# A routed FFN's tail: where three pairs of query tiles are normalised and their squared norms taken

## The reference

```python
q = (hidden_states @ Wq + bq).reshape(B, S, H, QD)      # 8 heads of 64
q = (q - mean) / jnp.sqrt(var + EPS_BN) * bn_gamma + bn_beta   # over all tokens and heads
q0 = _l2norm(q[..., :HALF]); q1 = _l2norm(q[..., HALF:])
s0 = jnp.einsum('bshq,kq->bshk', q0, k0); s1 = ...      # 32 keys each
ts0, ti0 = jax.lax.top_k(s0, 4); ts1, ti1 = jax.lax.top_k(s1, 4)
# 16 sums of a first and a second score, softmax over them: weights of 16 of 256 experts
eh = gelu(down[idx] . hidden_states)
out = sum over the chosen experts of up[idx] * eh * w
```

## Time and profile before

| what | value |
|---|---|
| time, median of 3 runs | 415.46 us (415.35 to 417.52) |
| the profiled execution | 416.85 us, its span 415.1 us |
| busy share: PE, DVE, ACT, POOL | 96%, 72%, 59%, 52% |
| the FFN's tail over the 16 tiles | about 331 to 413 us of the span |

### The profile page before, as it was taken

One profiled execution on the slowest core, in us unless ns is written; L12 is line 12 of the kernel. 1 busy time (PEld: TensorE's weight loads), 2 busy tenths in 40 slices (PEclk: granted clock), 3 DMA queues, 4 the chain that ended last, 5 costly groups with the idle time before them and its releaser, 6 DMA issues. The chain is left out here.

```text
span 415.1 us, 7901 instructions
## 1 busy us (share of the span) xinstructions
PE 397.8 (96%) x2582; PEld 367.0 (88%) x2582; DVE 297.7 (72%) x1104; ACT 245.7 (59%) x539; POOL 215.9 (52%) x208
## 2 busy tenths in 40 slices
PE   2999999999999999999999999999999999999877
PEld 1788888899899999999999999999778998999766
DVE  4889777786366676457565555565695999799996
ACT  3687759354465655456573534443566887779462
POOL 2588999764263224334333212000147767989994
PEclk9999999999999999999999999999999998999999
DMA  7800223003422222231232100000100000000101
GB/s 223 299 0 3 76 56 101 8 7 127 109 64 64 55 81 77 59 80 52 58 98 59 54 2 2 0 2 0 28 1 2 0 3 1 27 28 26 41 25 65
DMA packets 19993, 21.38 MB, mean 52 GB/s; under 512 B 3181, under 2 KB 16625, under 8 KB 19953
## 3 DMA queue, kind: packets, MB, share of 16 engines
q1 hardware_dynamic: 18832, 19.96, 16.4%
q10 hardware_dynamic: 1120, 0.92, 0.8%
HBM read 18.78 MB, written 2.10 MB: 50 GB/s over the span
## 5 line engine op out<-in xcount | busy, mean ns | idle before, releaser
L847 DVE TENSOR_TENSOR att_pTl<-context_pR,att_pTh 128x512 fp32r<-128x512 f32 x64 | 37.4, 586 | 26.4 <-ACT att_pTh L759 26.1
L1191 POOL TENSOR_TENSOR ffn_prod<-ffn_first,ffn_near 128x1024 f32<-128x1024 f32 (+1 forms) x29 | 54.1, 1882 | 2.1 <-DVE ffn_first L1608 2.1
L866 DVE TENSOR_REDUCE att_mx<-keep_pQ 128x1 f32<-128x402 f32 x64 | 35.3, 567 | 24.2 <-PE keep_pQ L77 24.2
L759 ACT ACTIVATE att_pTh<-context_pR 128x512 fp32r<-128x512 f32 x64 | 32.4, 516 | 9.8 <-PE context_pR L1018 9.0
L1762 PE MATMUL ffn_pT<-keep_ident,ffn_prod 128*128 128x128 f32 x240 | 29.5, 277 | 4.3 <-POOL ffn_prod L1191 4.3
L1762 PEld LDWEIGHTS ffn_pT<-keep_ident,ffn_prod 128*128 128x128 f32 x240 | 27.3, 143 | 6.5 <-DVE ffn_hT L1641 4.8
L223 POOL TENSOR_TENSOR gru_z<-gru_z,gru_g 128x512 f32<-128x512 f32 x16 | 28.8, 1801 | 8.0 <-DVE gru_g L428 8.0
L1018 PE MATMUL context_pR<-keep_ident,att_prob 128*128 128x128 f32 (+1 forms) x208 | 32.8, 272 | 0.0
L984 PE MATMUL context_pA<-context_cNh,att_pTh 128*128 128x256 f32 (+1 forms) x104 | 31.4, 301 | 0.8 <-DVE att_pTl L847 0.8
L984 PE MATMUL context_pA<-att_cNh,att_pTh 128*128 128x256 f32 (+1 forms) x104 | 31.1, 299 | 0.0
L759 ACT ACTIVATE att_vTh<-context_pR 128x256 fp32r<-128x256 f32 x16 | 6.1, 384 | 39.3 <-PE context_pR L1023 39.3
(11 more groups left out here) (332 smaller groups left out, 1307.9 us busy)
## 6 DMA issues: line engine op xcount, KB each, us to landing
keep_raw<-in_ctxT SPq DMA_DIRECT2D x24, 256.0 KB, 2.6
keep_raw<-in_ctx SPq DMA_DIRECT2D x24, 256.0 KB, 2.7
out<-keep_x SPq DMA_DIRECT2D x16, 128.0 KB, 1.7
keep_x<-in_x SPq DMA_DIRECT2D x3, 512.0 KB, 9.9
gru_wout<-in_W_out SPq DMA_DIRECT2D x1, 512.0 KB, 8.4
keep_raw<-in_fWq SPq DMA_DIRECT2D x2, 256.0 KB
keep_raw<-in_ctxT SPq DMA_DIRECT2D x8, 32.5 KB, 3.8
keep_raw<-in_ctx SPq DMA_DIRECT2D x4, 65.0 KB
```

What stands on the lines that cost most here:

```text
L759: act.activation(to, bank, ACT.Copy).then_inc(bank_high, 1)
L847: dve.tensor_tensor(to, bank, half(it, 0, n)[0].bitcast(F32), ALU.subtract).then_inc(bank_free, 1)
L866: last = dve.tensor_reduce(mx[:, h, j:j + 1], pS[:, j, 0:min(SPANS[j][1], CTX) - SPANS[j][0]], AX.X, ALU.max)
L1191: return eng.tensor_tensor(prod[:, i % PB, a:b].rearrange("p h (i j) -> p h i j", j=KEYS), (factor if factor is not None else first[:, n % ...
```

## The change

ScalarE: `normed` of pairs 5, 6 and 7 moves from the odd tile 2n+1, ahead of the squares, to the end of the even tile ahead of it (tiles 4, 6, 8), behind the leftovers. `normed(4)` and all of `squared` stay. TensorE: `norms` of pairs 5, 6 and 7 moves from the even tiles 6, 8, 10 to the odd tiles ahead of them (5, 7, 9), behind scores(7), scores(9), scores(11) and ahead of mix and sum_heads. Nothing is added or taken out.

```diff
                     if t == 1 and n + 3 < GROUPS:
-                        if n + 3 >= FIRST_ACT:
+                        if n + 3 == FIRST_ACT:
                             normed(n + 3)
                         squared(n + 3)
...
                         for j in range(1 if n == 1 else i - PER, i):
                             leftover(j)
+                    if t == 0 and FIRST_ACT < n + 3 < GROUPS:
+                        normed(n + 3)
...
-                    if t == 0 and 3 <= n + 2 < GROUPS:
+                    if t == 0 and 3 <= n + 2 <= FIRST_ACT:
                         norms(n + 2)
+                    if t == 1 and FIRST_ACT < n + 3 < GROUPS:
+                        norms(n + 3)
                     if WEIGH + 1 <= i:
                         mix(i - WEIGH - 1)
```

## The result

The changed kernel takes 424.9 us (423.89 to 425.44, 6 runs), the kernel before in the same comparison 416.48 (415.35 to 417.52, 6 runs): a ratio of 1.02, 95% interval 1.0174 to 1.0227, 8.4 us slower. Forecast was 421.2 with a range that ended at 423.8. The direction and the place were right, the size was not. The profiled execution has a span of 423.6 against 415.1, 8.5 more.

The account below looks back on a forecast made before the run. GpSimd (POOL) bounds the end, fed by VectorE, itself fed by a busy TensorE. Waits of 4.05 us plus 1.7 us for one clock fall make 5.75 us, added to 415.46: 421.2 us, range 418.0 to 423.8.

Parts of the forecast that it names:

- What bounds, and the way of the loss: TensorE's waits at norms(6) and norms(7) delay sum_heads, then VectorE's weigh, then POOL's back-to-back run: selected(11) 4.05 us late.
- Table load: ScalarE before exponentials(8): 1.28 us plus 0.1 for draining; with the skill's 1.38 us drain, a wait of 4.4 us.
- Pair 5, a gain of 0.65 us: Tile 6: VectorE's reciprocal starts at 358.6, not 359.29, so selected(6) and selected(7) follow 0.65 us earlier.
- The clock: TensorE falls to half clock once, behind the 3.0 us wait at norms(6), costed at 1.7 us.
- The sum: 4.05 us from the waits plus 1.7 us for one clock fall: 5.75 us slower.
- Pair 7: TensorE waits 1.7 us at norms(7), VectorE 2.4 us at weigh(6); selected(11) then starts 4.05 us late in all.
- The base: 5.75 us added to the median 415.46 us, taking the median execution to have the same stretches as the profiled one.
- The range: 8 in 10: 418.0 (no fall, waits a third shorter) to 423.8 us (two falls, each cutting 0.4 more).
- no change: POOL's slack at selected(8) takes up the delays of pairs 6 and 7, clock stays: about 415.5 to 417 us; chance 0.10.
- Faster: TensorE's waits are shorter and VectorE's cover holds: 414.1, at most 412.6 us; chance 0.08.

Follow-up runs that it names:

- the second profile: The changed kernel, unaltered, profiled once more: 424.7 us.
- The filler kernel: Changed kernel plus 7, 24 and 11 unused dense matmuls on TensorE ahead of norms(5), (6) and (7): 422.4 us, ratio 1.0146 against the kernel before.
- the kernel with the normed earlier: Against the changed kernel, normed of pairs 5, 6 and 7 one step further ahead on ScalarE, behind the squares of the pair before: 420.3 us, ratio 1.0095.
- ScalarE's half: Against the changed kernel, norms back at their old places on TensorE, normed of pairs 5 to 7 still early: 416.8 us, ratio 1.0004 against the kernel before.
- TensorE's half: Against the changed kernel, normed back in front of the squares, norms of pairs 5 to 7 still early: 429.6 us, ratio 1.031 against the kernel before.
- pair 6 alone: Against the kernel before, only pair 6 moved, in both queues; pairs 5 and 7 as before: 423.7 us, ratio 1.0157.

## Why the prediction was right and wrong

- *What bounds, and the way of the loss*: right. The waits at norms(6) and norms(7) were forecast as 3.0 and 1.7 us, measured 2.90 and 1.39 (2.91 and 1.40 in the second profile); "normed, table load, exponentials, squares in a row without a gap" is in the profile; VectorE's waits moved from the squared norms to `weigh`; both halves alone say the same.
- *Table load*: 1.28 us and the next row 0.02 behind its end. The drain of 1.38 us that the Trainium skill adds (ScalarE: Activation LUTs, What ACT_TABLE_LOAD costs) isn't there; with it the wait would have been the 4.4 us that the prediction gave for it, not 2.90.
- *Pair 5, a gain of 0.65 us*: it hangs on where the half clock lies. The steps of pair 5 were priced with TensorE at half clock up to 352.67 and whole behind it, as in the trace of before. In the first profile it came early at whole clock, waited 0.90 us at norms(5), and was at half clock behind it: from norms(5) to the end of `sum_heads(2)` 6.5 us (352.05 to 358.56) against 4.74. The gain was nothing (the reciprocal at 359.29 as before), mix(1) and all that follows it came 1.1 us late, and `norms(6)` began at 366.37, not 365.25. In the second profile the stretch lay at 350, there was no wait at norms(5), the reciprocal waited for the root as forecast and came 0.40 us sooner than before, and norms(6) was within 0.2 us of the forecast.
- *The clock*: the term of the sum that was mis-sized. It was "one fall there, costed at 1.7", the price of 3.4 us at half clock. Measured behind norms(6), in both profiles: 6.8 us at half clock, and in the first from the start of norms(6) to the end of `sum_heads(4)` 8.08 us (366.37 to 374.45) against 4.74, so 3.34 us. The filler kernel, 3.3 us shorter over the same steps, shows it by a run. Nor did both waits pay, as the prediction read the rule that it cites: no half clock followed the 1.39 us at norms(7) in either profile.
- *The sum*: `weigh(4)` was put at 2.15 + 1.7 = 3.85 us late and came 6.64 late. The excess of 2.8 is 1.1 (pair 5) + 1.64 (clock). Pair 7 then added 1.90, just what was forecast (4.05 less 2.15), though its wait was 1.39 and not 1.7; such a close agreement is in part luck. 6.64 + 1.90 = 8.54. In the second profile, counted from `selected(3)`, `weigh(4)` came 5.73 late, `selected(11)` 7.62: the clock's 1.64 is the same, the 1.1 is nearly absent.
- *The base*: the forecast was added to 415.46, the median of 3 runs. The same kernel took 416.48 in the comparison with the changed one. Of the 3.7 us between 421.2 and 424.9, 1.0 is that, and 2.7 the sum (8.4 against 5.75). The prediction took it that the median execution has the same stretch at half clock as the profiled one; the shape of the faster executions was not known.
- *The range*: its upper end allowed two falls of one length each, at pairs 6 and 7. It left out that a fall may last twice as long, or lie on the moved norms of pair 5, and it had nothing for a base 1 us off.
- *The rivals*: no change rested on slack at `selected(8)`, where POOL in fact waited 4.89 us. Faster needed a wait at norms(6) under 0.2 us; it was 2.90.

## What to carry to other kernels

Moving a step ahead in an in-order queue is safe only as far as its inputs have been made by then: from the last event that both engines wait on, add up the producer's way (a table load included) and the consumer's; the difference is the wait, and everything behind the moved step in its queue pays it. Where the waiting engine is TensorE, allow for half clock behind the wait as well, here 3.4 or 6.8 us of it, and look in more than one profile for where it falls. And before adding a forecast to a median of three runs, see whether the profiled execution is like the median one.

## What the runs showed of the hardware

In the fourteen profiles the half clock lasted 3.4 us in twelve stretches and 6.8 us in eight, with nothing between; two profiles have none. In the long ones too TensorE worked without a gap, on norms (4 columns), scores, mix and the transposes of `sum_heads`: 367.7 to 374.5 here, 353.7 to 360.5 in the kernel with the normed earlier. The Trainium skill (TensorE: Matmul & The Clock Gate, What's actually happening) has the clock return after sustained work; the work in these stretches did not bring it back at once.

What TensorE did when it fell: all eight long stretches began while norms ran. Of the twelve short ones ten began within 2 us behind the end of norms, one in their last 0.5 us, and one behind a wait of 1.92 us for GpSimd, far from any norms. That is a pattern in the rows, not a cause that a run tested. A wait is not needed for it. Six of the long ones began behind a wait, of 0.72 to 3.23 us, with the norms directly after it. The other two, in the kernels with one half of the change alone, began in norms(3), where TensorE had not waited since 311; ScalarE's half, from 337.6 to 344.5:

```profile
336.76 2.61 PE L1734 MATMUL ffn_pK<-ffn_group_of,ffn_sq 128*128 128x4 f32 x16
```

```profile
338.00:339.00 1.00, 1.00 (x6) 1.00 (x6) 0.00 (x0) 0.67 (x1) 0.04 (x1) 0.50 0.00 0
```

Nor does a wait alone cost the clock: the 1.39 us at norms(7) had no half clock behind it in either profile of the changed kernel, nor had 1.94 us in the kernel with TensorE's half alone. Behind all four waits of 2.9 us and more with norms after them it fell, for 6.8 us each time (two profiles of the changed kernel, TensorE's half, pair 6 alone). Dense matmuls in the wait prevented the fall at norms(6) in one kernel, halved it in another, and at norms(7) it fell in spite of them.
